# Taking 14 groups of dummy matmuls out of a two-layer decoder kernel

## What is computed

```python
x = _layernorm(x + _L0_attn_ref(x, ...))          # causal attention, 16 heads, latent width 32, rotary
x = _layernorm(x + _L0_xattn_ref(ctx_1024, x, ...)) # q @ (k^T v) per head, no softmax
x = _layernorm(x + _L0_ffn_ref(x, ...))           # blockwise FP4, 256 -> 704 -> 256, silu gate
x = _layernorm(x + _L1_attn_ref(x, ...))          # causal attention plus a second, moving-average part
x = _layernorm(x + _L1_xattn_ref(x, ctx_1024, mask, ...)) # masked cross attention, then 256 -> 1024 -> 256
x = _layernorm(x + _L1_ffn_ref(x, ...))           # blockwise FP6, 256 -> 256
```

## Time and profile before

| | us |
|---|---|
| median of 3 timed runs | 974.98 |
| lowest, highest | 974.42, 976.68 |
| profiled execution, whole time | 973.4 |
| its span, first to last instruction | 971.5 |
| PE busy | 847.3 (87%) |
| DVE busy | 766.7 (79%) |
| ACT busy | 639.1 (66%) |
| POOL busy | 303.3 (31%) |
| mean granted TensorE clock | 0.968 |

### The profile page before, as it was taken

One profiled execution on the slowest core, in us unless ns is written; L12 is line 12 of the kernel. 1 busy time (PEld: TensorE's weight loads), 2 busy tenths in 40 slices (PEclk: granted clock), 3 DMA queues, 4 the chain that ended last, 5 costly groups with the idle time before them and its releaser, 6 DMA issues.

```text
span 971.5 us, 29766 instructions
## 1 busy us (share of the span) xinstructions
PE 847.3 (87%) x11899; PEld 665.3 (68%) x11910; DVE 766.7 (79%) x1917; ACT 639.1 (66%) x2507; POOL 303.3 (31%) x554
## 2 busy tenths in 40 slices
PE   5577789999999998999999999989999999988863
PEld 4354567776777776767777777777677776766642
DVE  6977396889888888878887888888887879787552
ACT  3245458595968677695958586777859585855541
POOL 1112122233433324232433343342324333322122
PEclk9878899999999999999999999999999999999977
DMA  9200003000000000000000000000000000000000
GB/s 334 113 6 7 9 2 102 2 27 18 15 4 24 10 25 10 7 27 18 16 19 15 10 20 7 12 22 21 12 18 16 18 11 7 8 7 6 7 2 11
DMA packets 24442, 24.88 MB, mean 26 GB/s; under 512 B 2304, under 2 KB 22640, under 8 KB 24176
## 3 DMA queue, kind: packets, MB, share of 16 engines
q1 hardware_dynamic: 24304, 22.98, 7.2%
HBM read 18.80 MB, written 2.10 MB: 22 GB/s over the span
## 4 chain that ended last, share of the span: by engine, by line
PE 46%; DVE 25%; ACT 20%; issue 5%; POOL 3%; DMA 1%; DVEq 0%; SPq 0%; POOLq 0%
PE bank L1294 23%; PE s_tile L1294 19%; ACT prob L783 10%; DVE peak L1058 7%; DVE rope_ L1050 4%; ACT k_ L816 2%; DVE stats L1000 2%; ACT q_ L816 2%; DVE y_ L1013 1%; DVE y_ L1033 1%; DVE y_ L1036 1%; ACT xt_ L722 1%; ACT k_ L877 1%; POOL rstd L650 1%; PE s_tile L1415 1%
## 5 line engine op out<-in xcount | busy, mean ns | idle before, releaser
L783 ACT ACTIVATE prob<-s_tile,low 128x128 f32<-128x128 f32 x768 | 271.6, 403 | 18.2 <-DVE low L1063 18.2
L783 ACT ACTIVATION_READ_ACCUMULATOR prob<-s_tile,low 128x1 f32 x768 | 187.4, 244 | 0.0
L1058 DVE TENSOR_REDUCE peak<-s_tile 128x4 f32<-128x512 f32 x192 | 123.3, 684 | 31.7 <-PE s_tile L1294 31.7
L648 POOL TENSOR_TENSOR var_eps<-mean_var,rsq 128x1 f32<-128x1 f32 x144 | 31.6, 219 | 350.7 <-DVE mean_var L1002 350.5
L722 ACT ACTIVATE probT<-bank 128x512 f32<-128x512 f32 x192 | 99.5, 616 | 8.9 <-PE bank L1504 8.7
L650 POOL TENSOR_TENSOR rstd<-var_eps,rsq 128x1 f32<-128x1 f32 x144 | 84.0, 583 | 11.3
L1294 PE MATMUL bank<-w_gu,xt_ 128*128 128x352 f32 x256 | 82.6, 467 | 1.8 <-DVE y_ L1013 1.0
L1504 PEld LDWEIGHTS bank<-cst,prob 32*128 32x128 f32 x3072 | 54.9, 140 | 37.2 <-issue 17.6
L1504 PE MATMUL bank<-cst,prob 32*128 32x32 f32 x3072 | 61.1, 226 | 16.6 <-ACT prob L783 10.4
L1294 PEld LDWEIGHTS bank<-w_gu,xt_ 128*128 128x128 f32 x256 | 46.8, 189 | 32.6 <-DVE y_ L1013 9.0
L764 ACT ACTIVATE rope_<-bank,colt 128x128 f32<-128x128 f32 x64 | 18.3, 368 | 73.5 <-PE bank L1294 73.5
(11 more groups left out here) (212 smaller groups left out, 2003.0 us busy)
## 6 DMA issues: line engine op xcount, KB each, us to landing
xtin<-in_xT SPq DMA_DIRECT2D x16, 128.0 KB, 2.3
next_<-in_x SPq DMA_DIRECT2D x16, 128.0 KB, 2.2
ct_<-in_ctxT SPq DMA_DIRECT2D x16, 128.0 KB, 2.3
w<-in_w SPq DMA_DIRECT2D x2, 1024.0 KB, 9.6
out<-x_ SPq DMA_DIRECT2D x16, 128.0 KB, 1.7
next_<-x_ SPq DMA_DIRECT2D x16, 127.0 KB
rowt<-in_rows SPq DMA_DIRECT2D x1, 1664.0 KB, 9.0
w<-in_gate_up SPq DMA_DIRECT2D x2, 512.0 KB, 6.2
```

Of the source, the lines that this page charges most:

```text
L783: ins = act.activation(prob[:, r, c * P:(c + 1) * P], bank[r][:, c * P:(c + 1) * P], ACT.Exp, scale=SCALES[layer], bias=low[:, b, at0:at0 ...
L1058: dve.tensor_reduce(peak[:, b, 4 * r:4 * r + 4], rows4(src[:, :]), AX_X, ALU.max)\
```

## The change

The 14 stages are taken out: their names, their slots in TensorE's order, their banks, the helper `warm` and its entry in the table. The slots and banks of all real stages stay as they are. `COVERED` is written anew for the new sequence of fills: a few waits of TensorE on banks, which were needed because a dummy group had used the bank before, are now in the list of those left out.

```diff
-WARMS = [f"warm{n}" for n in range(14)]
-SETUP_STAGES += WARMS
...
 SLOTS = dict(
-        ... l0_scores=49406, warm0=49541, l0_mix0=49962, ...
-        ... f0_up2=51999, warm2=52365, f0_turn_h=52561, ...
-        ... x1_value=55595, warm1=55638, x1_out=55675, ...
-        f1_turn_x=58175, f1_out=58541, warm3=85795, warm10=85984,
-        warm8=86226, warm9=86436, warm4=86928, warm6=87464, warm11=87994, warm13=88007, warm12=89137,
-        warm7=90215, warm5=90664),
+        ... the same stages and slots without the warm ones
...
-BANKS: "p_warm0": 4, "p_warm1": 7, "p_warm2": 7, "p_warm3": 6, "p_warm4": 5, "p_warm5": 7, "p_warm6": 7,
-       "p_warm7": 0, "p_warm8": 6, "p_warm9": 0, "p_warm10": 6, "p_warm11": 7, "p_warm12": 6, "p_warm13": 5
...
-STAGE_FILLS.update({name: ["p_" + name] for name in WARMS})
...
-    ("l1_mix0", "free.t2"): (0, 14), ("l1_mix0", "free.t3"): (2, 15),
+    ("l1_mix0", "free.t2"): (0, 16), ("l1_mix0", "free.t3"): (0, 16),
-    ("x1_mix0", "free.t3"): (0, 14),
+    ("x1_mix0", "free.t2"): (14, 16), ("x1_mix0", "free.t3"): (0, 16),
+    ("x1_scores", "l1_ma.s0"): (0, 16),
-    ("x1_up2", "free.h1"): (0, 15),
+    ("x1_up2", "free.h1"): (0, 16),
+    ("x1_values", "free.v"): (14, 16),
...
-            def warm(name):
-                def f(i, b):
-                    dst = free(None, "p_" + name)
-                    for n in range(3):
-                        ins = mm(dst[:, :], ident_bf, bcst[:, P:P + 512])
-                    filled(ins, None, "p_" + name)
-                    emptied(mm(dst[:, :], ident_bf, bcst[:, P:P + 512]), None, "p_" + name)
-                return f
...
-            table.update({name: warm(name) for name in WARMS})
```

More of the change, by code:

```diff
@@ L73 @@
     PE=dict(v_bias=0, turn_up0=46719, l0_project=46970, turn_up1=47483, cproj_bias=48628, x0_kv=48970,
[L74 to L82, removed]
@@ L83 @@
-        x1_up2=56738, x1_down=56807, x1_down2=56831, f1_turn_x=58175, f1_out=58541, warm3=85795, warm10=85984,
-        warm8=86226, warm9=86436, warm4=86928, warm6=87464, warm11=87994, warm13=88007, warm12=89137,
-        warm7=90215, warm5=90664),
+        l0_lat=49033, turn_up2=49231, l0_latent=49337, l0_scores=49406, l0_mix0=49962, l0_mix1=49974,
+        l0_mix2=50034, l0_mix3=50047, l0_v=50248, l0_spread=50402, l0_value=50452, l0_out=50506, wo_bias=50595,
+        x0_mix=50765, turn_down1=50922, x0_turn_x=50950, x0_project=50983, turn_last=51064, x0_attend=51228,
@@ new lines @@
+        f0_turn_x=51816, f0_up=51894, f0_up2=51999, f0_turn_h=52561, f0_turn_h2=52692, f0_down=52717,
+        f0_down2=52719, l1_turn_x=53061, l1_project=53061, l1_scores=53178, l1_mix0=53630, l1_mix2=53645,
+        l1_mix1=53646, l1_mix3=53650, x1_keys=53691, l1_spread=53714, l1_value=53754, l1_ma=53789,
+        l1_back=53930, l1_ma_value=53970, l1_out=54202, x1_turn_x=54455, x1_project=54505, x1_scores=54722,
+        x1_values=55089, x1_mix0=55411, x1_mix1=55419, x1_mix2=55456, x1_mix3=55482, x1_spread=55582,
@@ L86 @@
+        x1_value=55595, x1_out=55675, x1_turn_h=56012, x1_up=56276, x1_up2=56738, x1_down=56807, x1_down2=56831,
+        f1_turn_x=58175, f1_out=58541),
     DVE=dict(quant_up0=0, columns=51, round_up0=1994, v_bias=4636, quant_up1=10992, round_up1=65248,
```

## The result

The changed kernel takes 985.18 us (median of four runs, 981.13 to 985.71); the kernel before, run beside it, 975.83 (four runs, 974.42 to 977.61). The ratio is 1.0085, 95% interval 1.0064 to 1.0105: slower, by about 8 us. Ratios and intervals here are worked out from all runs, so that they need not equal the quotient of two medians. The ratio times the 974.98 us shown ahead is 983.3 us; the median as measured, 985.18, lies 0.2 above the end of the forecast's range.

A forecast was written before the change was run, and what follows sets the result against it. Between 148 and 850 us TensorE works 657.7 of 702 us at full clock, so only head and tail can change. -0.6 + 3.3 + 2.1 = +4.8 on 973.4 gives 978.2, adjusted to 979.0 us; range 974 to 985.

The forecast's parts named there:

- Sign and mechanism: Whole kernel: slower, mainly because TensorE loses activity and the granted clock falls in the tail; slower was given 0.71.
- Direct part: Groups on the chain at 166.2, 882.2 and 935.4 us: leaving them out gives -0.6 us, bounds 0 and -3.4.
- Waits: About a dozen of TensorE's bank waits left out: 0 us, bounds 0 and 0.2 us gained.
- The three places: At 858, 892 and 905 us: clock falls at two of three, 2 x 1.63 = 3.3 us lost, bounds 0 and 8.9.
- The last stretch: Dense matmuls from 944.94 us begin at 1.2 GHz without the group at 942.0: 2.1 us lost, bounds 0 and 8.35.
- The head: Groups at 43 and 91 us: nothing taken for the clock, plus or minus 1.6 us.
- The sum: Whole kernel: -0.6 + 3.3 + 2.1 = +4.8 us on the profiled 973.4 us, so 978.2.
- From the profile to the median: Profiled execution 1.6 us below the median of the timed runs: about half added, giving 979.0 us.
- Only gaps count: Rival: clock holds at 858, 892 and 905 us, only the last stretch pays; 974.9 or 976.5 us, chance 0.18.
- Nothing but dead work: Rival: all groups are hidden and the clock moves as it does anyway; 975.0 us, chance 0.04.
- The faster rival: Groups' queue places at 166.2, 882.2 and 935.4 us cost; all 3.4 us comes back, 971.6 us, chance 0.09.
- The caveat at the prediction's end: Clock stretches may lie differently in each run; the kernel before then has such falls too and loses less.

The follow-up runs named there:

- 3: The kernel before with all 14 groups kept, each matmul streaming 8 columns instead of 512: 984.36 us, ratio 1.0077.
- 1: The kernel before with the head's three groups out and the tail's eleven kept: 975.3 us against 976.99, ratio 0.9999.
- 2: The kernel before with the tail's eleven groups out and the head's three kept: 982.32 us, ratio 1.0054.
- 5: The kernel before with only the nine groups from 853.9 to 919.1 us kept: 978.39 us against 976.84, ratio 1.0013.
- 4: The kernel before with only the last two groups (935.4 and 942.0 us) kept: 984.14 us, ratio 1.0079.
- 6: The kernel before plus 20 dummy matmuls at 928 us and 40 at 953: 974.7 us against 976.84, ratio 0.9982.
- 10: The kernel before without the five groups at 853.9, 855.2, 889.3 and 901.0 us (two), other nine kept: 980.12 us, ratio 1.0028.
- 7: The kernel before with the 43 us group at 22 matmuls, the 91 us group at 10, four head groups added: 974.53 us, ratio 0.9969.
- 8: The kernel before with added dummy matmuls both in the head and late (928 and 953 us): 971.23 us, ratio 0.995.
- 12: The kernel before with dummy work added in head, late and seven middle groups (five in bank 3, two in bank 4): 970.28 us against 976.04, ratio 0.9942.

## Why the prediction was right, and where its sizes were off

- **Sign and mechanism.** Right. The loss is the granted clock (the two traces); it comes from activity, neither from waits nor from order (3), and mostly from the tail (1, 2).
- **Direct part, -0.6.** The chain gave -0.21 at 882 (0.3 forecast) and nothing at 935 (0 forecast). At 166 the prediction gave the group 0.86, of which 0.3 pass: x1_out's y_ came 0.92 earlier (167.95 to 167.03) and cross_ 0.40 earlier (170.90 to 170.50), held by x0_kv as described; 0.07 of both was there already at 156 us, so that 0.85 and 0.33 are left. By 855 us this was gone again (+0.09); why isn't shown. So -0.1 in all.
- **Waits, 0.** Right within what can be measured: the hollow groups, with all waits kept, are as slow (3).
- **The three places.** The price of one fall, 1.63, was right: l1_project paid 1.63 exactly, the other two 1.58 and 1.90. The step that was off is the count, "I count two of the three": the clock fell at all three, 5.1 us for 3.3. There was no row for counting two; the busy shares that were worked out (2.0 of 4, 1.4 of 4, 2.2 of 5) were all like those ahead of the head's falls, and came out as 1.88, 1.11 and 1.98 of 4.
- **The last stretch, 2.1.** 2.73 in the traces, because the clock came back at 956 and not a few microseconds after 945. In timed runs the two last groups are worth less than that: leaving out them and the head's three costs 0.13% (-0.02 to 0.28) together (5), and without the middle ones nothing can be told of them (4). The prediction's 2.6 us for "at most double the first part" has no row (double the 4.44 would be 4.4 more), so that the 2.1 was a guess between it and 1.63 that came near.
- **The head, 0 with plus or minus 1.6.** Inside its bounds, but the 0 looks better than it is. The group at 91 us did shorten the low clock: without it the 12 matmuls of w_dn took 4.64 us for 2.97 (+1.7), as in every profile without it. The 24 at 103.8 took 2.96 for 4.59 (-1.6), but that fall at 104 stands in no other profile with the head's groups (2, 6, 10). Up to 150 us the changed kernel lost 1.40 us on its own start, and its profile had started 1.43 earlier: that the two cancel is luck. Over all profiles the head's groups are worth about 1.2 us, a term that the prediction put at nothing.
- **The sum.** +4.8 against the pair's +7.7: 1.8 for the third place, 0.6 for the last stretch, 0.5 for the direct part, and the head's +1.4 offset by the start's -1.4.
- **From the profile to the median.** The changed kernel's other runs are some 4 us longer than its profiled one, at a mean clock of 0.946 to 0.947 for 0.951. Where in the span these lie isn't shown; the longer stretches in 3 (7 us for 4 at 860) are a candidate, and the early start of the profiled run (1.43 us) another. The prediction added 0.8 for this.
- **Rivals.** "Only gaps count" fell: the clock fell behind waits of at most 0.88 us (860) and 1.71 us (908). At 894 a wait did grow past the rival's 1.6 us, to 2.60. The rule of the Trainium skill ("TensorE: Matmul & The Clock Gate", section "Why this matters for your kernels"), read literally as a question of one long gap, doesn't hold in this kernel; the advice of the same section to keep TensorE busy without a break for its full clock agrees with 6 to 8 and 12. "Nothing but dead work" fell with 3. The faster rival needed 3.4 us from its three places and got 0.33 (gone by 855), 0.21 and 0. The caveat at the prediction's end came true: the clock's stretches lie differently from run to run, in the kernel before as well (1, 6).

## What to carry to other kernels

Dummy matmuls in waits that exist anyway can pay, here 0.85% for 14 groups and up to 0.6% more, by keeping the granted clock up: place them where the dense work behind a thin stretch stands on the chain, and make them large enough (four matmuls at 43 us didn't keep the clock for the work behind the wait, 22 with some more behind them did). Put each in a bank that has long been read, or it becomes a wait itself. Judge such a change by many timed runs and by stretches of the granted clock over more than one trace, since where the clock falls in one trace is a draw. A profile also finds what the times can't: that the head's groups act was seen in one step of ten traces, and it is smaller than the noise of the medians.

## What was not expected of the hardware

- One kernel's time goes loosely with its mean granted clock from run to run. Of the 86 runs of the kernel before beside the experiments, the seven with a clock above 0.966 took 971.1 to 975.8 us (median 973.4), the 41 at 0.960 or less 975.5 to 982.3 (median 977.7).
- The falls lie at other places in other executions: with all the tail's groups in place the clock held from 148 to 933 in one trace, fell at 898 and 908 in another (1), and at 859, 900 and 910 in a third (6).
- More work on the busiest engine made the kernel shorter: with 98 matmuls added (8) the mean clock was 0.983, the span 968.2 and the time 970.09, 3.3 us below the profiled execution of before at 0.968.
